# Decoder layer with contextual positions: gate positions placed by ScalarE and GpSimd, turned outputs in a bank of their own, position logits ahead of the second logits

## The reference

```python
def _cope(q, sim, pos_emb):
    G = sigmoid(sim)
    P = flip(cumsum(flip(G)))               # gates summed from the last key backwards
    P = minimum(P, T_MAX - 1)               # T_MAX = 64
    E = einsum('bnc,ct->bnt', q, pos_emb)   # 64 position logits of each query
    w = P - floor(P)
    return w * E[ceil(P)] + (1.0 - w) * E[floor(P)]
sim = einsum('bid,bjd->bij', q, k) * scale
sim = sim + _cope(q, sim, pos_emb)
attn = softmax(sim)
out = einsum('bij,bjd->bid', attn, v)       # then heads side by side, @ Wout + b_out
```

## Time and profile before

| | before |
|---|---|
| median of 3 runs | 2650.29 us |
| the profiled execution | 2652.94 us, span 2651.1 us |
| busy shares of the span | PE 93%, DVE 76%, ACT 61%, POOL 7% |
| attention stage | from about 35 us to 2177 us of the span |
| mean granted TensorE clock | 0.985 of 2.4 GHz |

### The profile page before, as it was taken

One profiled execution on the slowest core, in us unless ns is written; L12 is line 12 of the kernel. 1 busy time (PEld: TensorE's weight loads), 2 busy tenths in 40 slices (PEclk: granted clock), 3 DMA queues, 4 the chain that ended last, 5 costly groups with the idle time before them and its releaser, 6 DMA issues. The chain is left out here.

```text
span 2651.1 us, 64197 instructions
## 1 busy us (share of the span) xinstructions
PE 2472.1 (93%) x18687; PEld 1691.1 (64%) x18687; DVE 2006.4 (76%) x5179; ACT 1615.9 (61%) x3383; POOL 190.4 (7%) x289
## 2 busy tenths in 40 slices
PE   7999998999899989998999999999999988999997
PEld 5666665666566656666666566666666656777776
DVE  6888888888888888888888888888899960232322
ACT  4666666666666666666666666666666663444442
POOL 0000000000000000000000000000000000111111
PEclk9999999999999999999999999999999998999998
DMA  2010101010101010100101110101001002100100
GB/s 68 20 33 20 34 20 32 20 34 20 32 20 34 20 32 21 32 21 21 29 24 29 25 29 24 29 24 29 22 21 40 21 17 68 34 26 34 36 26 6
DMA packets 96567, 74.74 MB, mean 28 GB/s; under 512 B 24590, under 2 KB 92303, under 8 KB 96464
## 3 DMA queue, kind: packets, MB, share of 16 engines
q1 hardware_dynamic: 96464, 73.15, 10.1%
HBM read 14.26 MB, written 2.10 MB: 6 GB/s over the span
## 5 line engine op out<-in xcount | busy, mean ns | idle before, releaser
L748 DVE TENSOR_REDUCE mx<-Sc 128x1 f32<-128x1024 f32 x512 | 621.5, 1214 | 160.2 <-PE Sc L544 159.7
L552 PE MATMUL ring<-ident,probs 128*128 128x128 f32 x4096 | 620.9, 284 | 115.2 <-ACT attn L418 65.3
L409 ACT ACTIVATE probsT<-ring 128x512 f32<-128x512 f32 x1024 | 584.7, 596 | 132.1 <-PE ring L552 129.2
L552 PEld LDWEIGHTS ring<-ident,probs 128*128 128x128 f32 x4096 | 446.3, 145 | 258.3 <-ACT attn L418 127.0
L430 ACT ACTIVATE probs<-Sc,nbias 128x1024 f32<-128x1024 f32 x512 | 565.6, 1117 | 4.7 <-DVE nbias L765 4.7
L544 PE MATMUL Sc<-qk,q_now 64*128 64x512 f32 x2048 | 539.4, 637 | 22.4 <-issue 16.0
L566 PE MATMUL out<-probsT,V_now 128*64 128x128 f32 x8192 | 530.0, 277 | 0.0
L566 PEld LDWEIGHTS out<-probsT,V_now 128*64 128x64 f32 x8192 | 439.5, 137 | 76.3 <-ACT probsT L409 57.9
L712 DVE COPY_PREDICATED z<-mask,z 128x224 f32<-128x224 int16 (+5 forms) x768 | 389.7, 507 | 34.4
L418 ACT ACTIVATE attn<-ring,rsum 128x64 f32 (+1 forms) x256 | 80.3, 314 | 436.5 <-PE ring L575 420.7
L544 PEld LDWEIGHTS Sc<-qk,q_now 64*128 64x128 f32 x2048 | 173.6, 188 | 217.8 <-issue 217.8
(11 more groups left out here) (116 smaller groups left out, 2301.8 us busy)
## 6 DMA issues: line engine op xcount, KB each, us to landing
q_now<-qk SPq DMA_DIRECT2D x256, 64.0 KB, 2.0
xv<-xT SPq DMA_DIRECT2D x113, 128.0 KB, 2.2
q_far<-qk SPq DMA_DIRECT2D x128, 64.0 KB, 1.9
V_now<-V SPq DMA_DIRECT2D x16, 512.0 KB, 3.2
at<-attn SPq DMA_DIRECT2D x16, 512.0 KB, 3.2
probs<-in_x_dram SPq DMA_DIRECT2D x4, 512.0 KB, 5.3
wqk<-in_L_attn_Wq_dram SPq DMA_DIRECT2D x32, 64.0 KB, 2.1
xin<-in_x_dram SPq DMA_DIRECT2D x16, 128.0 KB, 2.8
```

What stands on the lines that cost most here:

```text
L409: nc.scalar.activation(probsT[:, u, 4 * s:4 * s + 4, :], ring[k % 2][:, :].rearrange("p (t q) -> p t q", q=P), ACT.Copy).then_inc(slot_out, 1)
L552: last = nc.tensor.transpose(ring[k % 2][:, j * P:(j + 1) * P], probs[:, u, (4 * s + j) * P:(4 * s + j + 1) * P], ident[:, :])
L748: nc.vector.tensor_reduce(mx[:, u, half:half + 1], Sc[:, half * HALF:(half + 1) * HALF], AX.X, ALU.max).then_inc(dve_unit, 1)
```

## The change

- **Turned outputs.** The turn writes into a bank of its own, `turns`, no longer into the ring. It is issued between the second and the third slot of transposes (`transposes_and_turn`), and ScalarE scales it after all four slots are copied. A group has 10 slots, or 8 in the late groups.
- **The window.** The bank `near` is gone. The two window matmuls go into the two ring banks, one bank each; the second reads its keys from partitions 0 to 63 (`k_near`, filled by one more DMA per head), so that the two use different halves of the array. They are issued before the logits of unit 1, and wait until the ring is empty (`slot_out`). The transposes of unit 0 wait until both are copied out. ScalarE takes the tanh and copies the table (into `near_table_in`) right after the values.
- **Positions.** ScalarE places the positions with two activations, `rnd` (half of twoP plus 1.5 * 2^23, whose float32 rounding is the floor) and `rest` (Relu of 63 minus the position), between the scaled output and the exponentials of unit 1. GpSimd subtracts `rnd` from a ramp (`find_steps`), shifts `rest` (`find_rest`), forms the fractions (a cast and a difference), the products and the corrections, and copies the table into `z`. VectorE scans the steps with max into distances, makes seven masks and one more for the even part, does the last shift in one instruction, and no longer rounds, subtracts distances, clamps, or makes fractions and corrections. Its scans over the tanh stand before the reduction of the first half of unit 1's logits.

The halves' copy stands first, as before; the window's two copies follow the values. The core of the diff:

```diff
-SLOTS0 = 8 + 2 * PAIRS - 6
-SLOTS = 12
-LATE_SLOTS = 10
+SLOTS0 = 8 + 2 * PAIRS - 4
+SLOTS = 10
+LATE_SLOTS = 8
...
-    def __init__(self, first=False, proj=True):
-        self.turn0 = 0
-        self.last = [1, 2, 3, 4]
-        at = 6 if first else 5
-        self.qk, self.values = at, at + 1
...
+    def __init__(self, proj=True):
+        self.last = [0, 1, 2, 3]
+        self.qk, self.values = 4, 5
+        at = 6 if proj else 4
         self.now = [at, at + 1, at + 2, at + 3]
...
-        near = pb("near", [P, BANK])
-        ring = [pb(f"ring{i}", [P, BANK]) for i in range(2)]
+        rings = pb("rings", [P, 2, BANK])
+        ring = [rings[:, i, :] for i in range(2)]
         out = pb("out", [P, BANK])
+        turns = pb("turns", [P, BANK])
...
+            def find_steps(c):
+                pool.wait_ge(rounded, c + 1)
+                nc.gpsimd.tensor_tensor(steps[:, :, :], ramp[:, :, :], rnd[:, :, :],
+                                        ALU.subtract).then_inc(steps_done, 1)
+            def find_rest(c):
+                pool.wait_ge(rest_in, c + 1)
+                nc.gpsimd.tensor_tensor(rest[:, :, :], rest[:, :, :], ramp_rest[:, :, :],
+                                        ALU.add).then_inc(rest_done, 1)
+            def fractions(c):
+                pool.wait_ge(rest_done, c + 1)
+                wait_apart(pool, shifted, c * CH + (CHAIN.index("even") + 1), waited)
+                nc.gpsimd.tensor_copy(frac[:, :, :], even[:, :, :]).then_inc(even_in, 1)
+                pool.wait_ge(even_in, c + 1)
+                nc.gpsimd.tensor_tensor(frac[:, :, :], rest[:, :, :], frac[:, :, :],
+                                        ALU.subtract).then_inc(frac_done, 1)
...
+            def body(c):
+                fractions(c)
+                find_steps(c + 1)
+                products(c)
+                corrections(c)
+                start_table(c + 1)
+                find_rest(c + 1)
...
+            def positions(c, first=False):
+                act.wait_ge(scanned, c * SC + SC)
+                nc.scalar.activation(rnd[:, :, :], twoP[:, :, :], ACT.Identity, scale=0.5,
+                                     bias=bias_rnd[:, :]).then_inc(rounded, 1)
+                if not first:
+                    wait_apart(act, frac_done, c, waited)
+                nc.scalar.activation(rest[:, :, :], twoP[:, :, :], ACT.Relu, scale=-0.5,
+                                     bias=bias_rest[:, :]).then_inc(rest_in, 1)
...
                     empty_halves(g - 1, 0)
-                    scale(g - 1, 0, base, at.turn0)
                     transposed(1, base, at.last)
-                if near:
-                    act.wait_ge(corr_done, g + 1)
-                    near_table(g + 1)
+                    scale(g - 1, 0)
                 exps(g, 0)
                 if not first:
                     empty_halves(g - 1, 1)
...
+                if far:
+                    near_tanh(g + 2)
+                    near_table(g + 2)
+                transposed(0, base, at.now)
                 if not first:
-                    scale(g - 1, 1, base, at.turn1)
-                transposed(0, base, at.now)
+                    scale(g - 1, 1)
                 if far:
-                    act.wait_ge(scanned, g * SC + (SC + 2))
-                    near_tanh(g + 2)
+                    positions(g + 2)
                 exps(g, 1)
...
             def window(c, par):
-                pe.wait_ge(far_in, c * 16 + 16)
+                pe.wait_ge(far_in, c * 32 + 32)
                 for i in range(2):
-                    last = nc.tensor.matmul(near[:, i * (W + T):(i + 1) * (W + T)], q_far[C:P, i * P:(i + 1) * P],
-                                            qk[C:P, par, 1, HALF - W:QK], start=True, stop=True)
+                    rows = slice(0, C) if i else slice(C, P)
+                    keys = k_near[:, par, :] if i else qk[C:P, par, 1, HALF - W:QK]
+                    last = nc.tensor.matmul(rings[:, i, 0:W + T], q_far[rows, :], keys,
+                                            start=True, stop=True)
...
+            def transposes_and_turn(g, u, base, slots, turned_unit, first=False, evicted=True):
+                for s in range(4):
+                    transposes(u, base, slots, s)
+                    if s == 1 and not first:
+                        turn(g, turned_unit, evicted)
...
                 if not first:
                     outputs(g - 1, 1, base, at.last, tiles=range(FIRST, NT))
+                if far:
+                    wait_apart(pe, slot_out, base + at.now[0], waited)
+                    window(g + 2, par if far_par is None else far_par)
                 wait_apart(pe, exp_done, g * 4 + 1, waited)
                 logits(par, 1, 0)
                 wait_apart(pe, exp_done, g * 4 + 2, waited)
                 logits(par, 1, 1)
-                if not first:
-                    turn(g - 1, 1, base, at.turn1)
-                for s in range(4):
-                    transposes(0, base, at.now, s)
                 if far:
-                    pe.wait_ge(near_out, g * 2 + 4)
-                    window(g + 2, par if far_par is None else far_par)
+                    wait_apart(pe, near_out, g * 2 + 6, waited)
+                transposes_and_turn(g - 1, 0, base, at.now, 1, first)
                 outputs(g, 0, base, at.now, empty=not first)
...
+            def scan_distances(c):
+                dve.wait_ge(steps_done, c + 1)
                 for i in range(2):
+                    nc.vector.tensor_tensor_scan(dist[:, i, ::-1], steps[:, i, ::-1], ramp_top[:, ::-1], 0.0,
+                                                 ALU.max, ALU.max).then_inc(shifted, 1)
...
                     shift(c, 5)
+                    shift(c, 4)
+                if scan:
+                    scan_positions(c + 1)
                 half_max(g, 1, 0)
```

More of the change, by code:

```diff
@@ L200, in attention @@
         halves_out = sem("halves_out")
+        k_near_in = sem("k_near_in")
+        turned = sem("turned")
+        scaled = sem("scaled")
         summed = sem("summed")
@@ L277, in _, with body @@
             load_values(0)
[L279 removed]
+            def body(g, odd, late=False, first=False, tile=True, far=True, head=False, near=False):
                 base = slots_before(g, late)
[L281 to L284 removed]
                 if far:
@@ L352, in _ @@
+            pool.wait_ge(ramped, 4)
+            pool.wait_ge(dve_consts, 4)
+            start_table(0, first=True)
+            find_steps(0)
+            find_rest(0)
+            def body(c):
[5 more added lines that the diff above has]
+                find_rest(c + 1)
+            body(0)
+            with pool.Fori(1, G - 1) as c:
                 body(c)
+            fractions(G - 1)
@@ L354, in _ @@
+            products(G - 1)
+            corrections(G - 1)
         @block.scalar
@@ L590, in body @@
                 if not first:
-                    turn(g - 1, 0, base, at.turn0)
-                    for s in range(4):
-                        transposes(1, base, at.last, s)
+                    transposes_and_turn(g - 1, 1, base, at.last, 0, evicted=not second)
                     outputs(g - 1, 1, base, at.last, tiles=range(FIRST))
@@ L637, in _ @@
             pe.wait_ge(exp_done, 4 * G)
-            turn(G - 1, 0, base, at.turn0)
-            for s in range(4):
-                transposes(1, base, at.last, s)
+            transposes_and_turn(G - 1, 1, base, at.last, 0)
             outputs(G - 1, 1, base, at.last)
-            turn(G - 1, 1, base, 5)
+            turn(G - 1, 1)
         @block.vector
@@ L779, in add_halves, with body @@
                                         ALU.add).then_inc(summed, 1)
-            def body(g, late=False, first=False, chain=True, scan=True):
+            def body(g, late=False, first=False, second=False, chain=True, scan=True):
                 c = g + 1
@@ L785, in body @@
                 half_max(g, 0, 0)
-                if not first:
-                    corrections(g)
                 add_window(g, 0)
-                if chain:
-                    scan_floors(c)
                 window_max(g, 0)
                 bias(g, 0)
-                if chain:
-                    distances(c)
                 if not first:
@@ L797, in body @@
                 if chain:
-                    clamp(c)
+                    scan_distances(c)
                 if not first:
-                    invert(g - 1, 1, base)
+                    invert(g - 1, 1, used=not second)
                 if chain:
@@ L836, in _ @@
                 shift(0, b)
-            fractions(0)
             slopes(0)
             last_shift(0)
-            corrections(0)
             scan_positions(1)
-            round_positions(1)
+            saturation(1)
             body(0, first=True)
-            with dve.Fori(1, LASTP) as g:
+            body(1, second=True)
+            with dve.Fori(2, LASTP) as g:
                 body(g)
```

219 lines of the change are left out of this document (118 added, 101 removed).

## The result

The changed kernel took 2767.43 us (median of 4 runs, 2762.89 to 2769.64) against 2649.89 us for the kernel before in the same session: ratio 1.0441, 95% interval 1.0423 to 1.0459. The profiled execution has a span of 2767.8 us, 116.7 more than before.

A forecast was written before the change was run, and what follows sets the result against it. TensorE (93% busy) was nearly the bound, its loop balanced with one through tanh and exponentials. 111 x 1.4 + 8 x 1.2 + 1 = 166 us more gave 2819 by the profile, 2816 against the median; range 2760 to 2910.

The forecast's parts named there:

- stall ahead of the window: TensorE, after its outputs, stands 1.37 us through three ScalarE copies until the values' copy empties a ring bank.
- A to B: From the start of the first half's transposes to the start of the second half's: 10.0 us, was 8.63, +1.4.
- second exponentials behind B: The group's second exponentials start 4.5 us after the second half's transposes begin, as 4.48 before.
- rival of the covered wait: Values' copy ends before TensorE's outputs, so the window does not wait: group 15.2 us, 2483 us in all; chance 0.03.
- Two loops that end together: TensorE's own loop and that through tanh and exponentials end within 0.1 us, so making one shorter gives nothing.
- B to next A: From the second half's transposes to the next group's first: 8.0 us, change 0.0, scaling and placing taking the window's saving.
- cover: VectorE's nbias is ready at 13.3 us, ScalarE reaches the second exponentials at 14.5: 1.1 us of slack.
- last link: GpSimd's product and correction end at 17.4 us into the group, needed at 18.1: hidden with 0.7 over.
- a rival at 0.05: GpSimd instructions hold VectorE up ahead of nbias: +0.85 us per group, 2917 us in all; chance 0.05.
- Late groups: The 8 late groups without projection do not stall, as their ring is empty by 3.3: 15.2 us, change 0.
- the rival of the clock: TensorE's new waits put one set of logits per group at 1.2 GHz: +1.8 us, 3030 us; chance 0.03.
- Prologue: Before the steady groups, the chain through two more engines adds 1 us.

The follow-up runs named there:

- Kernel 1: The changed kernel with ScalarE copying the other unit's output halves behind the projection and values instead of ahead: 2625.18 us, ratio 0.9918 to the kernel before.
- kernel 5: The changed kernel with both window matmuls in the same half of the array, still in two banks: 2811.53 us, ratio 1.0622 to the kernel before.
- kernel 4: The kernel before with only the turn moved to free columns of the output halves' bank, issued between second and third transpose slots: 2490.77 us, ratio 0.9413.
- kernel 6: The changed kernel with one more VectorE reduction (1.2 us) ahead of the nbias for the second exponentials: 2807.65 us, ratio 1.0616 to the kernel before.
- kernel 2: The changed kernel with the two placements ahead of the four copies of transposes instead of ahead of the exponentials: 2724.36 us, ratio 1.0294 to the kernel before.
- kernel 7: The changed kernel with GpSimd's cast and difference for the fractions over one column in all groups but the first: 2755.84 us, ratio 1.0411 to the kernel before.

## Why the prediction was right, and where it was off

The direction, the mechanism and the range held: 2767 lies in 2760 to 2910, near its lower end. The move was 117.5 us where 166 were forecast. Step by step:

| step, us per group | forecast | measured |
|---|---|---|
| transposes and turn, each half | 2.6 | 2.42 |
| stall ahead of the window | 1.37 | 1.56 |
| window | 0.57 | 0.51 |
| A to B | 10.0 | 9.93 |
| two placements | 0.9 | 0.96 |
| second exponentials behind B | 4.5 | 4.18 |
| exponentials to next A | 3.5 | 3.49 |
| group | 18.0 | 17.60 |

- **A to B.** Right within 0.1, but by errors that cancel: the transposes were 0.18 shorter, the stall 0.19 longer, since the way back from the values' copy to TensorE took 0.30 (1005.22 to 1005.52) where I had 0.05. Kernel 1 shows that the stall is the halves' copy, kernel 5 that the window is on the path. The rival of the covered wait was summed wrongly: its 15.2 takes the 1.4 off twice. 18.0 - 1.4 is 16.6, no change at all, and kernel 1, which removes most of the stall, measured 16.34.
- **Two loops that end together.** "Making one shorter gives nothing" holds for an edit that touches only one of them. Both contain a run of transposes, and the turn by itself took 0.74 off A to B and 0.58 off B to A (kernel 4).
- **B to next A.** The mis-sized term is here: exponentials at B + 4.5, measured 4.18. Half of the 0.32 is the shorter run of transposes, and the rest that the last copy and the scaled output follow each other closer than I added them: the copies' pair ends at B + 3.13 instead of 3.3, the scaled output had begun by then, and the placements follow 0.2 behind its start. Over 111 groups this is 36 of the 48 us that the forecast was too high by; A to B gives another 8. The other parts nearly cancel, which is luck: the late groups (+8.5) and the prologue (+6.2) against the edges of heads (about -9), the end (-5.6) and the groups without values (-3.8).
- **VectorE.** nbias at B + 3.3, as forecast (A + 13.3, measured 1011.16 - 997.91 = 13.25); cover 0.86 forecast at 1.1, measured by kernel 6.
- **GpSimd.** Its last link was "hidden with 0.7 over" in the forecast; measured, nothing is over. In the steady groups the correction ends at A + 17.95, and VectorE's add that uses it starts 0.03 behind (0.14 behind the reduction ahead of it). So it was only just in time. That it holds VectorE up was a rival at 0.05; the hold-up exists (kernels 2 and 7) but was paid only once the placements had been moved away, and in the late groups.
- **Late groups: this step failed.** "They do not stall, 0" was right about the ring and wrong about the group: 8.5 us more. There VectorE has no slack to absorb what GpSimd costs it. The timeline of a late group of the changed kernel:

```profile
2192.30 0.93 POOL L377 TENSOR_TENSOR steps<-ramp,rnd 128x352 f32<-128x352 f32 x1 [5.48 <-ACT rnd L476]
2192.59 1.04 DVE L816 COPY_PREDICATED z<-mask,z 128x344 f32<-128x344 int16 x1
2193.54 0.14 DVE L851 TENSOR_REDUCE nbias<-mx 128x1 f32<-128x2 f32 x1
2193.71 1.11 ACT L526 ACTIVATE probs<-Sc,nbias 128x1024 f32<-128x1024 f32 x1 [1.00 <-DVE nbias L851]
...
2195.06 3.67 PE L645 MATMUL Sc<-qk,q_now 64*128 64x512 f32 x8 [2.25 <-ACT probs L526]
```

A shift takes 1.04 us beside GpSimd's steps, nbias is late by 1.00 us, TensorE waits 2.25 us, and the logits then run at the 1.2 GHz level (3.67 us for eight passes, 2.23 in the steady part). The granted clock over 2165 to 2275 us was 0.91, and 1.00 in the late groups before. This is the rival of the clock, confined to six groups (the last two, which have no window, are faster than before). The forecast's argument against it, "waits of 1 us around 1000 us", misread the rows: a steady group of the kernel before had 0.9 us of waits in pieces, of which the earlier trace rows shows 0.35. How the late groups' time divides can be read from kernel 7, where the masks are short and the two costs come apart. Its logits in three late groups, of 14.39, 15.51 and 16.91 us:

```profile
2171.30 2.22 PE L645 MATMUL Sc<-qk,q_now 64*128 64x512 f32 x8 [1.13 <-ACT probs L526]
...
2186.81 2.22 PE L645 MATMUL Sc<-qk,q_now 64*128 64x512 f32 x8 [2.25 <-ACT probs L526]
...
2216.78 3.39 PE L645 MATMUL Sc<-qk,q_now 64*128 64x512 f32 x8 [2.25 <-ACT probs L526]
```

In the first the exponentials do not wait for nbias; in the other two they wait 1.00 us. So the late nbias costs 1.1 us and the slow logits another 1.4. All six groups of the changed kernel (16.9 us) have both. By these numbers its order alone would give 14.4, 0.9 less than the 15.3 of before. The forecast's 15.2 was too long for the order, and had neither of the two costs.
- **Prologue.** +1 was forecast, +7.2 came. ScalarE's placements of group 1 stand ahead of the last projection's copies and waited 4.60 us for VectorE's scans, which stand behind the whole first chain; the ring stayed full meanwhile, and TensorE's first logits came at 37.3 instead of 30.7. The queue behind a new wait was not followed there:

```profile
35.50 0.59 ACT L476 ACTIVATE rnd<-twoP,bias_rnd 128x352 f32<-128x352 f32 x1 [4.60 <-DVE twoP L784]
...
36.83 0.37 ACT L457 ACTIVATE V<-rings 128x256 f32<-128x256 f32 x1
...
37.34 3.31 PE L645 MATMUL Sc<-qk,q_now 64*128 64x512 f32 x8 [4.37 <-ACT V L457]
```

- **Edges of heads.** Not in the forecast: about 9 us given back. Perhaps the groups that wait there have less to lose; no run tests it.

## What to carry to other kernels

When an engine takes a new wait in front of its longest work, follow the releasing engine's queue back to its first instruction: here it waited for the very engine that was made to wait, and swapping copies in that queue was worth about 140 us. Try the parts of a change one by one: the turned output's place alone made the kernel 5.9% faster, and a group of the changed kernel takes 2.3 us more than one of that kernel. A loop that ends within 0.1 us of another still gives room if the edit shortens a stretch that both contain, as the transposes are.

## What the runs showed of the hardware that was not expected

- An Identity or a Relu of 352 float32 elements from SBUF took 588 and 584 ns on ScalarE (0.48 us from start to start), a tanh of the same size out of PSUM 464. The first two also take a bias from a tile and the tanh does not; no run separates the two.
- Instructions of VectorE beside one of GpSimd took longer (seven masks 1.21 to 2.23 us, slopes 0.52 to 1.04, a two-element minimum 0.15 to 0.62), while its reductions out of PSUM stayed at 1.2 us. The minimum of kernel 2 ended 0.03 us behind GpSimd's difference (1003.02 and 1002.99).
- TensorE's waits of 1.56 and 1.13 us in every group of 17.6 left the granted clock at 0.99; a single wait of 2.25 us per group of 16.9 went with 0.91 and logits at half speed. It does not always: one of the three late groups with that wait in kernel 7 kept its logits at 2.22 us.
